# Attention sums beside eight experts: another order of work on PE and VectorE

## The reference, cut to what matters

```
x = x + gnn(layernorm(x))          # 4 heads of 64
    ft = h @ W;  e = leaky_relu(e_src[src] + e_dst[dst])
    a = exp(e - segment_max(e)) / segment_sum(...) * dist
    out = segment_sum(ft[src] * a, dst)
x = x + ffn(layernorm(x))          # 8 experts, all of them for every node
    w = softmax(mean_over_batch_of_one(x) @ Wr + br)
    h = relu(bn(x @ W1)); h = relu(bn(h @ W2)); y = h @ Wo + bo
    sum over experts of y * w
```

## Time and profile before

| | before |
|---|---|
| median of the runs | 1632.74 us |
| profiled execution | 1626.42 us |
| its span | 1624.6 us |
| PE busy | 1500.8 us, 92% |
| VectorE busy | 1227.3 us, 76% |
| GpSimd busy | 1019.9 us, 63% |
| ScalarE busy | 742.7 us, 46% |
| mean granted clock of PE | 0.978 |
| chain that ended last | PE 59%, VectorE 17%, issue 11%, ScalarE 6% |

### The profile page before, as it was taken

One profiled execution on the slowest core, in us unless ns is written; L12 is line 12 of the kernel. 1 busy time (PEld: TensorE's weight loads), 2 busy tenths in 40 slices (PEclk: granted clock), 3 DMA queues, 4 the chain that ended last, 5 costly groups with the idle time before them and its releaser, 6 DMA issues.

```text
span 1624.6 us, 24122 instructions
## 1 busy us (share of the span) xinstructions
PE 1500.8 (92%) x8458; PEld 1301.8 (80%) x8458; DVE 1227.3 (76%) x2301; ACT 742.7 (46%) x1292; POOL 1019.9 (63%) x951
## 2 busy tenths in 40 slices
PE   6927999899999899999999999999999999999998
PEld 5726888778788688888888888888888888888887
DVE  8735677778678588788888878878887887888751
ACT  4501343444345354555445544554554545544553
POOL 3176666767677667667767766766766776677000
PEclk9958999999999899999999999999999999999999
DMA  9785344343444433434444343444434344343000
GB/s 236 194 241 175 93 129 117 100 130 92 131 115 108 124 97 105 127 111 119 112 122 111 105 126 108 107 125 108 125 106 126 107 107 123 110 117 92 21 3 11
DMA packets 106069, 187.49 MB, mean 115 GB/s; under 512 B 38357, under 2 KB 70490, under 8 KB 105919
## 3 DMA queue, kind: packets, MB, share of 16 engines
q0 software_dynamic: 44688, 123.13, 28.2%
q1 hardware_dynamic: 60701, 62.29, 13.3%
q10 hardware_dynamic: 560, 0.52, 0.1%
HBM read 172.72 MB, written 14.42 MB: 115 GB/s over the span
## 4 chain that ended last, share of the span: by engine, by line
PE 59%; DVE 17%; issue 11%; ACT 6%; another core or an unknown queue 4%; DMA 2%; SPq 1%; ACTq 0%; POOL 0%; DVEq 0%
PE bankH L830 29%; PE bankY L859 13%; DVE gath L1423 4%; PE bankE L783 3%; PE bankB L761 3%; PE bankE L784 3%; ACT msg_hi L994 3%; ACT h L1022 3%; DVE onehot L1384 3%; PE bankE L776 2%; DVE msg_lo L1429 2%; DVE x L1498 2%; DMA table<-gath 1%; DVE x L1441 1%
## 5 line engine op out<-in xcount | busy, mean ns | idle before, releaser
L675 POOL DMA_INDIRECT gath<-table,src_win x900 | 999.4, 1110 | 442.2 <-issue 228.7
L1022 ACT ACTIVATE h<-bankH,bn_shift,bn_scale 128x250 f32<-128x250 f32 x800 | 401.8, 553 | 440.6 <-PE bankH L830 324.7
L859 PE MATMUL bankY<-wo,h 128*125 128x256 f32 x1600 | 380.8, 381 | 11.7 <-issue 10.1
L830 PE MATMUL bankH<-h,w 128*128 128x250 f32 x1600 | 382.3, 381 | 1.0 <-ACT h L1022 0.6
L830 PE MATMUL bankH<-xT,w 128*128 128x250 f32 x1600 | 374.4, 376 | 3.7 <-issue 2.5
L859 PEld LDWEIGHTS bankY<-wo,h 128*125 128x125 f32 x1600 | 295.4, 188 | 60.1 <-issue 18.9
L830 PEld LDWEIGHTS bankH<-xT,w 128*128 128x128 f32 x1600 | 297.4, 191 | 36.7 <-issue 3.1
L830 PEld LDWEIGHTS bankH<-h,w 128*128 128x128 f32 x1600 | 297.2, 191 | 36.6 <-issue 2.0
L1429 DVE TENSOR_TENSOR msg_lo<-gath,msg_hi 128x2340 fp32r<-128x2340 f32 x89 | 231.4, 2600 | 79.5 <-issue 50.5
L1498 DVE SCALAR_TENSOR_TENSOR x<-bankY,gate,x 125x256 f32<-125x256 f32 x400 | 174.1, 477 | 131.1 <-PE bankY L859 100.0
L994 ACT ACTIVATE msg_hi<-gath 128x2340 fp32r<-128x2340 f32 x89 | 191.7, 2154 | 173.6 <-DVE gath L1423 75.8
(11 more groups left out here) (190 smaller groups left out, 995.2 us busy)
## 6 DMA issues: line engine op xcount, KB each, us to landing
onehot_t<-dst_low SPq DMA_DIRECT2D x48, 576.0 KB
gath<-table,src_win POOLq DMA_INDIRECT x900
x_res<-in_x SPq DMA_DIRECT2D x25, 250.0 KB
out<-x SPq DMA_DIRECT2D x25, 250.0 KB
table<-gath SPq DMA_DIRECT2D x25, 227.5 KB
w<-in_L_ffn_W SPq DMA_DIRECT2D x8, 512.0 KB
gath<-in_x SPq DMA_DIRECT2D x5, 672.0 KB
wo<-in_L_ffn_Wo SPq DMA_DIRECT2D x4, 512.0 KB
```

Source lines behind the costliest of these rows:

```text
L675: pool.indirect_dma_start(gath[:, g.slot(u), t, :], None, table, bass.IndirectOffsetOnAxis(src_win[:, g.win, u, t:t + 1], 0)).then_inc(row ...
L830: mm = pe.matmul(target[:, hc * 2 * NT:(hc + 1) * 2 * NT], weights[:, e * KC + c, hc * P:(hc + 1) * P], operand(c), start=(c == 0), stop=( ...
L859: mm = pe.matmul(bankY[0:NT, u * D:(u + 1) * D], h2[:, e % 2, c, u, :], wo[:, e * KC + c, :], start=(c == 0), stop=(c == KC - 1))
L1022: ins = act.activation(target[:, e % 2, hc, :, :].rearrange("p u n -> p (u n)"), source[:, hc * 2 * NT:(hc + 1) * 2 * NT], ACT.Relu, bias= ...
```

## The change

On PE `turn_carry` goes from ahead of the second layer to behind it. On VectorE, step 0 starts with the maxima, ahead of edge sum and gates; in other steps they come behind `place`. `carries` stays in front, but `logits` goes behind the low part. `add_y` goes ahead of both residuals. The residual of tile 0 moves from step 5 to step 6 in most plans, the one-hot of chunk 2 from step 6 to 7. `weigh` of a pass waits for the next step where the next step also ends a pass. Pairs 4 and 5 get two passes (steps 0 and 2), pairs 6 to 9 two passes (steps 0 and 1) where there was one; pair 1 gets one split chunk, pairs 4 and 5 all four. Pair 0 gets more matmuls of `stay_busy`. The lists `early`, `full` and `BEHIND` and the number `DENSE` are not in the diff.

```diff
@@ class Plan
+    def weighs(self, s):
+        if not self.ends(s) or self.begins(s):
+            return []
+        return (self.ends(s - 1) if self.begins(s - 1) else []) + self.ends(s)
...
-NEXT = {4: (0,), 5: (1,), 6: (2,), 7: (3,)}
-STEADY = Plan(FOUR, new=2, onehots=NEXT, residuals={5: (0,), 6: (1,)}, passes=((0, (0, 1)),), low=ALL)
+NEXT = {4: (0,), 5: (1,), 7: (2, 3)}
+SPLIT = {1: (0,), 2: (1,), 4: (2,), 5: (3,)}
+STEADY = Plan(FOUR, new=2, onehots=NEXT, residuals={6: (0, 1)}, passes=((0, (0, 1)),), low=ALL)
+PLANS = {0: Plan({2: (0,), 3: (1,), 6: (2,), 7: (3,)}, place=2, new=6, rows=6, onehots={3: (0, 1), 8: (2, 3)},
+                 residuals={3: (0,), 7: (1,)}, passes=((0, (0,)), (4, (1,))), turn=8),
+         1: Plan({3: (0,), 4: (1,), 6: (2, 3)}, new=6, rows=6, onehots={6: (0, 1), 7: (2, 3)},
+                 residuals={6: (0, 1)}, passes=((1, (0,)), (4, (1,))), low=(1,))}
+for n in (2, 3):
+    PLANS[n] = Plan(FOUR, new=5, rows=5, onehots=NEXT, residuals={6: (0, 1)}, products=SPLIT, passes=((0, (0,)), (3, (1,))), low=(0, 1, 3))
+for n in (4, 5):
+    PLANS[n] = Plan(FOUR, new=4, rows=4, onehots=NEXT, residuals={6: (0, 1)}, products={1: (0,), 3: (1,), 4: (2,), 5: (3,)}, passes=((0, (0,)), (2, (1,))), low=ALL)
+for n in (6, 7, 8, 9):
+    PLANS[n] = Plan(FOUR, new=3, onehots=NEXT, residuals={6: (0, 1)}, passes=((0, (0,)), (1, (1,))), low=ALL)
@@ PE, turn_x1
+                stay_busy(g, 4)
@@ PE, body
-                    for k, tiles in plan.ends(s):
-                        turn_carry(g, k)
-                        stay_busy(g, 12)
...
                     if run and (s >= 1 or not f.begins(1)):
                         layer2(*before(f, s, 1), nothing)
+                    for k, tiles in plan.ends(s):
+                        turn_carry(g, k)
+                        stay_busy(g, 12)
...
-                                stay_busy(g, 8)
+                                stay_busy(g, 8 if c < 2 else 14)
@@ VectorE, logits
+                if found(g, k) > 1:
+                    dve.wait_ge(ex_ready, found(g, k) - 1)
@@ VectorE, body
-                    if g is not None and not g.begins(1) and s == 0:
-                        edge_sum(g)
+                    if s == 0:
+                        for k, tiles in plan.begins(s):
+                            runs(g, k, tiles)
+                        if g is not None and not g.begins(1):
+                            edge_sum(g)
                     for k, tiles in plan.ends(s):
                         carries(g, k)
-                        logits(g, k)
...
+                    for k, tiles in plan.ends(s):
+                        logits(g, k)
+                    if a is not None and s == plan.place:
+                        place(a)
+                    if s > 0:
+                        for k, tiles in plan.begins(s):
+                            runs(g, k, tiles)
...
+                    if run and (s >= 2 or not f.begins(1)):
+                        add_y(*before(f, s, 2))
+                    if 0 in plan.residuals.get(s, ()):
+                        residual(g, 0)
                     if a is not None:
                         for c in plan.onehots.get(s, ()):
                             make_onehot(a, c)
-                    for k, tiles in plan.begins(s):
-                        runs(g, k, tiles)
-                    if run and (s >= 2 or not f.begins(1)):
-                        add_y(*before(f, s, 2))
+                    if 1 in plan.residuals.get(s, ()):
+                        residual(g, 1)
+                        norm1(g, 0)
+                        norm1(g, 1)
...
-                    for k, tiles in plan.ends(s):
+                    for k, tiles in plan.weighs(s):
                         weigh(g, k, tiles)
+                    if plan.ends(s):
                         for c in plan.products.get(s, ()):
                             messages(g, c)
```

More of the change, by code:

```diff
@@ L87, with __init__ @@
 class Plan:
-    def __init__(self, sums, place=1, bounds=3, new=1, rows=3, onehots=None, residuals=None, products=None, passes=(), low=()):
+    def __init__(self, sums, place=1, bounds=3, new=1, rows=3, onehots=None, residuals=None, products=None, passes=(), low=(), turn=7):
         self.sums, self.place, self.bounds, self.new, self.rows, self.onehots = sums, place, bounds, new, rows, onehots
-        self.residuals, self.passes, self.low, self.turn = residuals, passes, low, 7
+        self.residuals, self.passes, self.low, self.turn = residuals, passes, low, turn
         self.products = products or {s - 1: chunks for s, chunks in sums.items()}
@@ L106, in ends @@
         return self.begins(s - 1)
+    def weighs(self, s):
+        if not self.ends(s) or self.begins(s):
+            return []
+        return (self.ends(s - 1) if self.begins(s - 1) else []) + self.ends(s)
 ALL = tuple(range(CHUNKS))
 FOUR = {3: (0,), 4: (1,), 5: (2,), 6: (3,)}
-NEXT = {4: (0,), 5: (1,), 6: (2,), 7: (3,)}
-NONE = Plan({})
-STEADY = Plan(FOUR, new=2, onehots=NEXT, residuals={5: (0,), 6: (1,)}, passes=((0, (0, 1)),), low=ALL)
-PLANS = {0: Plan({2: (0,), 3: (1,), 5: (2,), 6: (3,)}, place=2, new=5, rows=5, onehots={3: (0, 1), 7: (2, 3)},
-                 residuals={3: (0,), 6: (1,)}, passes=((0, (0,)), (3, (1,)))),
-         1: Plan({3: (0,), 4: (1,), 6: (2, 3)}, new=6, rows=6, onehots={4: (0,), 6: (1,), 7: (2, 3)},
-                 residuals={6: (0, 1)}, passes=((1, (0,)), (4, (1,)))),
-         2: Plan(FOUR, new=5, rows=5, onehots=NEXT, residuals={5: (0,), 6: (1,)},
-                 products={1: (0,), 2: (1,), 4: (2,), 5: (3,)}, passes=((0, (0,)), (3, (1,))), low=(0, 1, 3)),
-         3: Plan(FOUR, new=5, rows=5, onehots=NEXT, residuals={5: (0,), 6: (1,)},
-                 products={1: (0,), 2: (1,), 4: (2,), 5: (3,)}, passes=((0, (0,)), (3, (1,))), low=(0, 1, 3)),
-         4: Plan(FOUR, new=4, rows=4, onehots=NEXT, residuals={5: (0,), 6: (1,)},
-                 products={1: (0,), 2: (1,), 3: (2,), 4: (3,)}, passes=((0, (0,)), (2, (1,))), low=ALL),
-         5: Plan(FOUR, new=3, onehots=NEXT, residuals={5: (0,), 6: (1,)}, passes=((1, (0, 1)),), low=(1, 2, 3))}
@@ L1548, in body @@
                             messages(g, c)
-                    if a is not None and s == plan.place:
-                        place(a)
                     if a is not None and s == plan.new:
                         new_runs(a)
-                    if g is not None:
-                        for u in plan.residuals.get(s, ()):
-                            if u == 0:
-                                residual(g, u)
+                    if run and (s >= 2 or not f.begins(1)):
+                        add_y(*before(f, s, 2))
+                    if 0 in plan.residuals.get(s, ()):
+                        residual(g, 0)
                     if a is not None:
```

8 lines of the change are left out of this document (1 added, 7 removed).

## The result

The changed kernel took 1655.08 us (median of 4, 1651.14 to 1658.82) against 1631.66 for the kernel before (4 runs beside it, 1622.00 to 1635.06): ratio 1.0153, 95% interval 1.0103 to 1.0203, slower by 1.5%. The forecast was 1610, faster. The profiled execution took 1651.14 us for a span of 1649.4, 24.8 more than the span of before. Medians and ranges here are over all executions of a kernel; the ratios leave out those more than 1.5% above its fastest (one of p_before, four of the ten of t_step6).

What follows compares the result with a forecast made beforehand. The prediction took PE's own list of matmuls to set the end, with the time to win being PE's waits. Its terms, -19.4-0.5+13.9-10-3.5-1.7-1.8, summed to -23.0, so 1632.7 became 1610 us; range 1597 to 1628.

Steps and rivals of the forecast that it cites:

- the start of the expert sum of step 7: Start of late stages on VectorE: sum starts at 0.2 us, in four of fourteen stages 1.7 after the stage's start.
- f9 to f22: Fourteen late stages: ten win 1.8 less 0.1 for slips, four about 0.6, together -19.4 us.
- Slower: VectorE's list from step 7 to the row maxima becomes PE's bound in every stage: +13, 1646 us; chance 0.13.
- first layer of expert 0: Pair 0: more filler matmuls keep the full clock for this layer, 1.85 in place of 3.64: -1.8 us.
- pair 1's split: Pair 1: one sum over 9 columns is split, 2.24 us in place of 4.11: -1.7 us.
- f1, f2: Stages of pairs 2 and 3: low part ahead of logits removes the wait at the second sum: -10 us.
- f3, f4: Stages of pairs 4 and 5, two passes: 59.7 us each in place of 62.2 and 61.9, together -3.5.
- f5 to f8: Stages of pairs 6 to 9, one pass turned into two: about 61.1 us each, together +13.9.
- Step 6: Late stages: third layer and sum over edges stop waiting, second layer waits 0.35: 1.04 us won a stage.
- The seam: Step 0 of late stages: PE's transposes find the maxima ready at 6.0 us: 0.76 won a stage.
- half clock: Two-pass stages: the waits of 2.35 and 2.8 drop the clock four to six times, +8 to +10, 1619 us; chance 0.12.
- split passes cost nothing: Stages of pairs 6 to 9: the step 1 wait only moves step 3's, costing 1 us each, 1600 us; chance 0.10.

Runs made afterwards that it cites:

- p_before: The kernel before, unchanged, run again with a profile on chip 0: 1598.28 us.
- t_step6: The kernel before with only step 6 in the new order, on chip 4: 1653.59 us, ratio 1.0085 to the kernel before.
- d4: The changed kernel with TensorE's signal for expert 5's third layer delayed, on chip 15: 1643.99 us, ratio 1.0280 to the kernel before.
- p_after: The changed kernel, run again with a profile on chip 0: 1581.26 us, ratio 0.9898 to the kernel before.
- s2: The kernel before with only step 6 in the new order, on chip 0: 1582.50 us, ratio 0.9902 to the kernel before.
- s1: The changed kernel with the turned carries back ahead of the second layer, on chip 0: 1597.68 us, ratio 0.9998 to the kernel before.
- e1: The changed kernel with SP's load of the second half of onehot_t about 20 us earlier, on chip 5: 1583.04 us, ratio 0.9897 to the kernel before.
- e3: The changed kernel with pairs 6 to 9 again in one pass, on chip 5: 1558.41 us, ratio 0.9742 to the kernel before.
- e2: The changed kernel with step 7's two one-hots ahead of the expert sum, on chip 5: 1583.21 us, ratio 0.9900 to the kernel before.
- after: The changed kernel in the timed pair: 1655.08 us, ratio 1.0153 to the kernel before.
- r_after: The changed kernel once more, on chip 7: 1665.57 us, ratio 1.0228 to the kernel before.
- r_all: The changed kernel with load early, one-hots first and one pass for pairs 6 to 9, on chip 7: 1631.96 us, ratio 0.9993 to the kernel before.
- t_best: The changed kernel with one pass for pairs 6 to 9 and for pair 5 (found at step 1), on chip 4: 1633.17 us, ratio 1.0013 to the kernel before.
- d5: The kernel before with TensorE's signal for expert 5's third layer delayed, on chip 15: 1641.92 us, ratio 1.0272 to the undelayed kernel.

## Why the prediction was wrong, step by step

The failed step is the start of the expert sum of step 7: "Sum from 0.2 to 1.0", in four of fourteen stages 1.7, ten late stages winning 1.7 and four 0.6. I took these starts from the trace of before and kept them for the new order. The runs showed 2.7 to 4.2 in every late stage of the timed profile, and f9 to f22 account for 38.5 of the 42.3 us between the timed difference (+24.8) and the one on chip 0 (-17.5). What followed from it was in the rival "Slower": VectorE's list from step 7 is the bound, and slip is paid nearly in full. Its price is measured by d4: 2.74 for 2.99. I gave it 0.13, because I counted slip as queueing on VectorE; in p_after there is none. (Its 1.3 us of slip in each stage is where the gain is used up, 18x1.3 = 23, not where slower begins.) The earlier trace rows had the warning: 2.86 idle "<-remote" at 769.94, a release that nothing in the profile explains, and I read it as a fixed 1.7 that belongs to four of the fourteen stages.

The terms, from two pairs of profiles; chip 0 (p_before, p_after) tests the counting, the timed pair what it met. The forecast's -1.8 (first layer of expert 0) and -1.7 (pair 1's split) both stand in f0; the rows are rounded:

| term | forecast | chip 0 | timed pair |
|---|---|---|---|
| until f0 begins | 0 | -1.1 | +1.1 |
| f0 | -3.5 | -3.6 | -1.5 |
| f1, f2 | -10 | -4.2 | -3.5 |
| f3, f4 | -3.5 | +0.6 | -0.3 |
| f5 to f8 | +13.9 | +17.6 | +17.4 |
| f9 to f22 | -19.4 | -26.2 | +12.3 |
| f23 | -0.5 | -0.6 | -0.6 |
| sum | -23.0 | -17.5 | +24.8 |

- *Late stages.* Step 6 was forecast at -1.04 and is -0.92 (s2), the sum over edges at 47.3 after the stage's start and is at 741.06-693.6 = 47.5. The seam was forecast at -0.76 and is -0.95. The counting holds where the signals are in time; the stages take 55.58, at the lower edge of the forecast band.
- *The place of the turned carries* is a condition for it: back ahead of the second layer they cost 1.45 a late stage (s1). In the two-pass stages it is the other way round: with the carries ahead f5 to f8 take 59.2 to 59.4, with them behind 61.4 to 63.0.
- *Two passes.* The waits were forecast at 2.35 and 2.8 and are 2.14 and 2.64 idle (2.23 and 2.81 by spacing) in p_after and in e1. From the base of 55.6 two passes cost 5.8 to 8.8 a stage (e1 against e3), 25 us together. Without them the change is worth 41 us on such a chip (e3), with them 16.
- *f1, f2.* The wait of 3.66 in the earlier trace rows is gone, as forecast (the sum for f1 adds up to 59.7, not 59.4; -10 stands either way). But in p_before that wait is 1.60, and f1 and f2 are at 59.9 and 59.7: more than half of what I took for a cost of the old order was the chip's.
- *f3, f4.* f4 is worse by 2.4 on chip 0 (58.0 to 60.4), where I had it 2.2 better: its 61.9 in the earlier trace rows held 3.9 of late signals, of which I had counted some 2.
- *f6.* I called its 10.8 "a hold of PE that no line of the change touches", and warned that it could come back elsewhere. It is the same cause: the first layer of expert 0 signalled at +6.65.
- *Rival "half clock".* After waits of 2.1 to 2.7 in f5 to f8, one stage of four in e1, in e2 and in p_after lost the clock for a while (64.36, 62.94 and 62.99 against 61.4): 3.0, 1.5 and 1.6, once in each, not four to six times. In the timed pair three of the four, f5, f6 and f8, show 0.97.
- *Rival "split passes cost nothing"* is refuted by e3.

What stays open is why TensorE's signals are late on chips 4 and 7. Between the timed profile of before and p_before the means in the late stages are the same (TensorE's matmul records 331 ns in both, packets of the gather 165 and 164 ns, VectorE's operations 620 ns and ScalarE's 687 in both), the matmuls run on at full pace while their signals wait, and most releases come in steps of about 1.4 us (1.3 to 1.4, 2.7, 4.1, 5.5, 7.0 after the stage's start, a few between them at 2.0 and 3.4). Neither SP's load nor the place of the two one-hots makes them. In the late stages of the kernel before the signal of expert 5 comes at 0.2 to 1.75 on such chips, in each kernel with the new step 6 (after, r_after, r_all, t_best, t_step6) at 1.3 to 4.2, in most of them at 2.7. Why the order moves it is not settled: t_step6 points to step 6 as enough for it, not to how, and the kernel before has no trace on its chip 4.

The Trainium skill (Perfetto Trace Analysis, Tensor Engine Instruction) says that a matmul's end in a profile is estimated, and that the signal goes out only once PSUM has acknowledged all bytes. The traces agree that the update comes behind the record's end, and show how far the two can part: under 0.02 us on chips 0, 5 and 15, up to 5.2 in the late stages on 7 and up to 7.9 in f6 of t_step6 on 4. What an update waits for they do not show.

## What to carry to other kernels

Before trusting a wait in a profile, compare the time of the semaphore update with the end of the record that makes it; a release put down to "remote", or a wait whose releaser ended long ago, may be a property of that run, and a plan counted from such a trace counts the chip in. A list that stands behind a cross-engine signal at a stage's seam should keep slack for it: here each us of lateness beyond the slack cost 0.9 us of a stage (2.74 for 2.99 in d4, where there is next to no slack; 1.38 for the 1.5 beyond the hidden 1.5 in d5's stages at full clock). And a gain of 1% needs its pair of kernels on more than one chip: the sign of this one changed between chips 0 and 7.

## What the runs showed of the hardware that I had not expected

- TensorE's semaphore updates can come microseconds after the matmul's end (up to 5.2 in late stages, 7.9 in f6 of t_step6) while the engine goes on at full pace; VectorE's and ScalarE's are on time throughout in the same traces. In all six profiles from chips 4 and 7 and in both of the timed pair over a hundred are late, in the twelve from chips 0, 5 and 15 none. The disturbed traces also record fewer updates: 829 to 851 of TensorE's against 1022 to 1034, and fewer of VectorE's and ScalarE's too, so their counts are lower bounds.
- The same kernel differs between chips 0 and 7: the kernel before by 2.2% of its time (1632.47 against 1597.04) and the changed one by 5.3% (1665.57 against 1581.26).
- The length of a wait alone does not tell whether the half clock follows: f6, f7 and f8 of p_after, with waits of 2.1 to 2.7, kept 1.00 granted and f5 was at 0.97; in d5 a wait of 1.96 was followed by it in six of fourteen late stages.
